# Layer-1 attention output computed transposed, with V stationary in two column halves

## The chip, the cores and the metric

The kernel runs on one core of one Trainium2 chip. The time is that of one execution on the device, in microseconds (us). Lower is better. The kernel before takes 1022.87 us, the median of three runs (1020.79 to 1023.86).

## The reference, cut to what matters

Two transformer layers on x of shape (32, 128, 128): cross-attention and a feed-forward part in each. The change touches the second attention (layer 1) and, at one place, the feed-forward part behind it.

```python
def _L1_xattn_ref(x, context, mask, ...):
    h, d = 16, 64; scale = h ** (-0.5)
    xn = _ln(x, ln1_s, ln1_b); cn = _ln(context, lnc_s, lnc_b)
    q = xn @ Wq; k, v = jnp.split(cn @ Wkv, 2, axis=-1)        # to 16 heads of 64
    k = concatenate(null_kv[0], k); v = concatenate(null_kv[1], v)
    sim = einsum('bhid,bhjd->bhij', q * scale, k); sim = where(mask, sim, -max)
    attn = softmax(sim, axis=-1)
    out = einsum('bhij,bhjd->bhid', attn, v) -> (b, n, 1024)
    return _ln(out @ Wo, lno_s, lno_b)

x = x + _L0_xattn(_layernorm(x), ctx); x = x + _L0_moe_ffn(_layernorm(x))
x = x + _L1_xattn_ref(_layernorm(x), ctx, mask, ...)
x = x + _L1_ffn(_layernorm(x))        # gate, up, down with quantised weights and activations
```

There is one null key and value ahead of the 128 keys of each sequence, so a softmax runs over 129 entries.

## The kernel before

All four parts run on one core, written by hand engine by engine; semaphores tie the engines together. Layer 0 (attention with routing, then the experts) takes the first 400 us or so. The rest is `attention_ffn_block` (from L1080), which this change is in. Its tensors have 128 partitions; one iteration b handles one sequence of 128 rows, and the engines run ahead of each other: iteration b does scores and softmax of sequence b, prepares queries and keys of b + 1, writes out the attention of b - 1, and does the feed-forward part of sequence f = b - 3.

The order of the work on each engine is fixed by the loops at the end of `tensor_part` (PE, L1593), `scalar_part` (ACT, L1708), `vector_part` (DVE, L1914), `pool_part` (POOL, L1333) and `sync_part` (SP's DMA queue, L1228). An engine does its list strictly in turn, so an instruction that waits holds all behind it.

PSUM has eight banks. Two (`maxp`) take the low-precision scores for the row maxima, two (`tp`) the scores proper, two (`op`) the product of the softmax with V, and the last two, `pa` and `pb`, are shared by all that remains: queries, keys, values, transposes, gate, up, down and output. Who may write `pa` or `pb` next is told by waits, such as this one in `queries(b, half)` (L1438), whose second half writes `pb`, which `gate_multiply(b - 4)` reads as its second operand:

```python
            elif b >= 4:
                pe.wait_ge(gt_ready, b - 3)
```

The attention of one sequence goes as follows. `scores` (L1506) leaves keys on partitions and rows of x along the free axis, for 8 heads at a time, in pairs that use the upper and the lower half of the rows of PE's array. `exps` on ACT turns them into `pT`. `weighted` (L1521) multiplies for each head with pT as the stationary operand (128 x 128) and V of this head with a mask column behind it as the moving one (65 columns); the extra column is the sum over keys. `normalise` on DVE (L1784), in three chunks of heads, adds the null entry `pn`, takes the reciprocals of 6, 5 and 5 sums and multiplies. The result `oh` has rows of x on partitions, so `o_transposes` on PE (L1420) turns it by 8 transposes, `o_copy` on ACT (L1671) moves it to `oT`, and `output` (L1471) multiplies by Wo. The weights of the null entry take a transpose (L1415) and a copy (L1652) of their own. `null_scores` (L1463) is the score of the null key, one small matmul into bank `op[0]`.

In the feed-forward part, `gate_part` (L1553) writes `pb`, `gate_tanh` on ACT (L1687) and `gate_multiply` on DVE (L1870) read it; `up_part` writes `pa`, read by `multiply`; then `h_range`, `h_scale` on ACT, `h_round` on DVE (L1893) and `h_transposes` on PE (L1571), `h_copy` and `down`. `quantise_x` (L1853), `out_norm` (L1813), `stats` (L1737) and `norm` (L1750) are small 128 x 128 steps of DVE. `k_copy` (L1759) moves half the keys out of PSUM. Layer 0's product with V (`values`, L365) has 32 columns of V stationary and writes four heads into four quarters of the partitions.

## Time and profile before

| | before |
|---|---|
| median of three runs | 1022.87 us |
| the profiled execution, its own time | 1026.15 us |
| its span | 1024.3 us |
| PE busy | 946.9 us (92%) |
| PE weight loads | 775.3 us (76%) |
| DVE busy | 724.9 us (71%) |
| ACT busy | 464.1 us (45%) |
| POOL busy | 405.9 us (40%) |
| mean granted clock of PE | 0.97 |

The busy time of PE is the union of its matmuls; they are pipelined, so the duration of one record overlaps the next, and what counts is the distance between starts. An f32 matmul leaves two records, a bf16 matmul and an f32 transpose one. Shapes such as 128*64 behind a tile are the part of the array (rows * columns) that holds the weights. "Idle before" with an arrow names what released the engine.

### The profile page before, as it was taken

The page shows a single profiled execution, that of the slowest core. Times are in us where ns is not written, and L with a number is a line of the kernel's source. Part 1 is how long each engine was busy: PE and PEld are TensorE (multiplying, and loading weights), DVE is VectorE, ACT ScalarE, POOL GpSimd, SP SyncE. Part 2 cuts the span into 40 slices and gives each one's busy share as a digit, 9 for nine tenths or more (in the row PEclk, how much of TensorE's full clock was granted, in tenths as well). Part 3 has the DMA queues.
Part 4 walks back from the last instruction along what each step waited for, and adds up shares of the span by engine and source line. Part 5 has one row for each costly group of instructions (what it writes and reads, how often), then busy time and mean ns, then how long its engine had stood idle before and what let it go on. Part 6 is the DMA issues. An engine that isn't in the chain of part 4 may idle for free.

```text
span 1024.3 us, 27291 instructions
## 1 busy us (share of the span) xinstructions
PE 946.9 (92%) x9480; PEld 775.3 (76%) x9510; DVE 724.9 (71%) x2240; ACT 464.1 (45%) x1073; POOL 405.9 (40%) x993
## 2 busy tenths in 40 slices
PE   4999999999689994899999999999999999999973
PEld 2677776777578884788888888888888888888851
DVE  2577777777543553668888788888878878788764
ACT  1355454454325652343545445444454544445432
POOL 3243467655632224242434435343343434434121
PEclk9999999999889997899999999999999999999995
DMA  8555400000355663000000000000000000000000
GB/s 218 179 200 199 171 18 18 12 8 12 98 153 153 165 160 86 12 12 7 9 17 10 17 9 16 11 9 17 10 17 9 10 17 9 17 10 7 4 6 8
DMA packets 47880, 54.23 MB, mean 53 GB/s; under 512 B 6658, under 2 KB 32642, under 8 KB 47746
## 3 DMA queue, kind: packets, MB, share of 16 engines
q1 hardware_dynamic: 33746, 28.43, 10.3%
q10 hardware_dynamic: 11952, 19.86, 5.2%
q0 software_dynamic: 2048, 4.20, 1.4%
q8 instruction: 78, 1.28, 0.5%
q14 instruction: 56, 0.46, 0.2%
HBM read 28.36 MB, written 24.12 MB: 51 GB/s over the span
## 4 chain that ended last, share of the span: by engine, by line
PE 89%; DVE 4%; issue 2%; SPq 2%; DMA 1%; ACT 1%; POOL 1%; DVEq 0%; POOLq 0%; ACTq 0%
PE psum L1548 11%; PE psum L354 7%; PE psum L1512 7%; PE psum L1460 6%; PE psum L1452 6%; PE psum L1493 6%; PE psum L1478 5%; PE psum L872 4%; PE psum L361 4%; PE psum L1517 3%; PE psum L371 3%; PE psum L862 3%; PE psum L1434 3%; PE psum L1502 2%; PE psum L344 2%
## 5 line engine op out<-in xcount | busy, mean ns | idle before, releaser
L1548 PE MATMUL psum<-a_v,a_pT 128*128 128x65 f32 x1024 | 124.1, 274 | 0.1
L1548 PEld LDWEIGHTS psum<-a_v,a_pT 128*128 128x128 f32 x1024 | 119.7, 192 | 1.2
L468 ACT ACTIVATE l_pT<-psum 128x512 f32<-128x512 f32 x128 | 69.7, 595 | 71.7 <-PE psum L361 71.5
L589 DVE TENSOR_REDUCE l_mx<-psum 128x4 bf16<-128x512 f32 x128 | 82.1, 683 | 12.8 <-PE psum L344 12.0
L1317 POOL TENSOR_TENSOR f_hd<-f_hmc,f_wmean 128x1 f32<-128x1 f32 x32 | 6.1, 192 | 197.3 <-DVE f_hr L1891 197.3
L1775 DVE TENSOR_REDUCE a_mxf<-psum 128x4 f32<-128x512 f32 x128 | 81.2, 676 | 0.0
L1460 PEld LDWEIGHTS psum<-a_cTm,a_Wk 128*128 128x128 f32 x512 | 63.4, 195 | 21.7 <-issue 21.7
L1664 ACT ACTIVATE a_pT<-psum 128x512 f32<-128x512 f32 x128 | 69.5, 599 | 20.7 <-PE psum L1517 20.7
L1452 PEld LDWEIGHTS psum<-a_xT,a_Wq 128*128 128x128 f32 x512 | 66.2, 196 | 16.3 <-issue 14.8
L354 PE MATMUL psum<-l_qz,l_kT 32*128 32x256 f32 x512 | 76.2, 417 | 0.0
L1512 PE MATMUL psum<-a_qT,a_kT 64*128 64x128 f32 x1024 | 75.3, 287 | 0.0
L1763 DVE TENSOR_TENSOR a_kT<-psum,a_nkm 128x512 f32<-128x512 f32 x64 | 44.0, 688 | 40.4 <-PE psum L1460 40.4
L1460 PE MATMUL psum<-a_cTm,a_Wk 128*128 128x128 f32 x512 | 72.4, 286 | 0.0
L1452 PE MATMUL psum<-a_xT,a_Wq 128*128 128x128 f32 x512 | 70.8, 283 | 1.1 <-ACT a_cT L1648 1.1
L1674 ACT COPY a_oT<-psum 128x512 f32<-128x512 f32 x64 | 37.4, 585 | 75.6 <-PE psum L1434 75.6
L1512 PEld LDWEIGHTS psum<-a_qT,a_kT 64*128 64x128 f32 x1024 | 62.9, 189 | 10.6 <-issue 10.5
L1493 PE MATMUL psum<-a_Wv,a_cTm 128*128 128x512 f32 x128 | 67.3, 608 | 0.6 <-DVE f_x L1903 0.5
L1478 PE MATMUL psum<-a_Wo,a_oT 128*128 128x128 f32 x512 | 63.2, 277 | 3.4 <-DVE f_h L1880 3.4
L1478 PEld LDWEIGHTS psum<-a_Wo,a_oT 128*128 128x128 f32 x512 | 60.3, 193 | 3.7 <-issue 3.7
L1684 ACT COPY a_v<-psum 128x512 f32<-128x512 f32 x64 | 37.5, 586 | 53.8 <-PE psum L1493 53.8
L354 PEld LDWEIGHTS psum<-l_qz,l_kT 32*128 32x128 f32 x512 | 45.7, 192 | 12.8 <-issue 4.8
L831 POOL COPY e_w2t<-e_w 128x512 f32 x39 | 23.8, 614 | 75.6 <-PE psum L872 75.6
(289 smaller groups left out, 2212.0 us busy)
## 6 DMA issues: line engine op xcount, KB each, us to landing
sorted_x<-r_zeros ACTq DMA_DIRECT2D x12, 1408.0 KB, 5.5
e_w<-in_E_W1b SPq DMA_DIRECT2D x39, 258.0 KB, 2.8
e_xt<-sorted_x SPq DMA_DIRECT2D x39, 64.0 KB, 2.3
sorted_y<-e_yt ACTq DMA_DIRECT2D x39, 64.0 KB, 2.3
a_cin<-in_ctx SPq DMA_DIRECT2D x32, 64.0 KB
out<-f_x SPq DMA_DIRECT2D x32, 64.0 KB, 1.7
x_res<-in_x SPq DMA_DIRECT2D x1, 512.0 KB, 5.8
l_cT<-in_ctxT SPq DMA_DIRECT2D x1, 512.0 KB, 7.0
```

What stands on the lines that cost most here:

```text
L354: nc.tensor.matmul(tp[e][:, 2 * n * S:2 * (n + 1) * S], kT[r, s, :], qz[r, s, 2 * n:2 * n + 2, :].rearrange("p h q -> p (h q)"), start=(n ...
L468: nc.scalar.activation(pT[:, k, :], tp[k % 2], ACT.Exp, scale=SCALE).then_inc(exp_ready, 1)
L589: nc.vector.tensor_reduce(mx[:, s, Q4 * k:Q4 * k + Q4], maxp[k % 2].rearrange("p (h t) -> p h t", h=Q4), AX_X, ALU.max).then_inc(mx_ready, 1)
L1452: last = nc.tensor.matmul(bank[:, i * S:(i + 1) * S], Wq[:, 4 * half + i, :], xT[:, b % 2, :], start=True, stop=True)
L1460: last = nc.tensor.matmul(bank[:, i * S:(i + 1) * S], Wk[:, 4 * half + i, :], cTm[:, b % 2, :], start=True, stop=True)
L1478: nc.tensor.matmul(pa[:, 0:D], oT[:, p, :], Wo[:, p, :], start=(p == 0), stop=False)
L1493: nc.tensor.matmul(bank, cTm[:, b % 2, :], Wv[:, 512 * half:512 * half + 512], start=True, stop=True).then_inc(v_done, 1)
L1512: nc.tensor.matmul(tp[e][:, i * S:(i + 1) * S], kT[r, b % 2, p, :], qT[r, b % 2, p, :], start=(i == 0), stop=False, skip_group_check=True)
L1548: mm = nc.tensor.matmul(op[c][:, k * VW:k * VW + HD + 1], pT[:, hh // 4, (hh % 4) * S:(hh % 4 + 1) * S], v[:, b % 2, hh, :], start=True, s ...
L1664: nc.scalar.activation(pT[:, 2 * half + e, :], tp[e], ACT.Exp, scale=SCALE).then_inc(exp_ready, 1)
L1763: nc.vector.tensor_tensor(kT[:, b % 2, 4 * half:4 * half + 4, :], (pa, pb)[half].rearrange("p (n k) -> p n k", n=4), nkm[:, b % 2, :].unsq ...
L1775: nc.vector.tensor_reduce(mxf[:, hh:hh + 4], maxp[e].rearrange("p (h t) -> p h t", h=Q4), AX_X, ALU.max).then_inc(mxf_ready, 1)
```

## The change

- `weighted`: V of a head (128 x 64) is now stationary and pT (128 columns) moves; the even and the odd group of heads go to the lower and the upper 64 partitions of one bank, so the output comes out transposed. V loses its mask column. `o_transposes`, `o_copy`, the transpose of `wn` and its copy are gone. Wo is loaded with its rows in the order of the new layout.
- `sums`: 16 matmuls with a mask block of 32 columns stationary sum pT over keys into four quarters of the partitions, 4 more transpose the null entries `pn`. Both go to a corner of bank `maxp[0]`.
- `null_copy` on ACT, and `inverse` on DVE (an add and a reciprocal of 128 x 128).
- `spread` on SP: the 16 rows of reciprocals are stored to DRAM and loaded back to all partitions (two DMAs of 256 KB).
- `normalise` on DVE is now two multiplications of 128 x 512, one iteration later, ahead of `gate_multiply`.
- POOL takes over the residual add, the rounding of h and the null weights. `null_scores` moves to another bank and place. On SP's queue, context tiles are loaded and outputs stored behind `spread`.

```diff
@@ tiles
-    v = sb("v", [P, 2, H, HD + 1])
+    v = sb("v", [P, 2, H, HD])
+    mask_sel = sb("mask_sel", [P, 2, Q4, Q4 * G])
-    dn, pn = sb("dn", [P, H]), sb("pn", [P, H])
+    dn, pn = sb("dn", [P, H]), sb("pn", [P, H, G])
+    nullT, denT, rT = sb("nullT", [P, S]), sb("denT", [P, S]), sb("rT", [P, S])
+    r_all = sb("r_all", [P, 2, Q4 * S])
+    denP, nullP = maxp[0][:, 0:S], maxp[0][:, S:2 * S]
+    r_rows = nc.dram_tensor("a_r_rows", (H, S), F32, kind="Internal").ap()
@@ SP
+        def spread(b):
+            sp.wait_ge(inverse_seq, 2 * b + 2)
+            if b >= 1:
+                sp.wait_ge(r_spread, 32 * b)
+            sp.dma_start(r_rows, rT[0:P:G, :]).then_inc(r_stored, 16)
+            sp.wait_ge(r_stored, 16 * (b + 1))
+            if b >= 1:
+                sp.wait_ge(oT_ready, 2 * b)
+            for e in range(2):
+                rows = r_rows.rearrange("(a e i) q -> e a (i q)", a=2, e=2)[e]
+                sp.dma_start(r_all[e * HD:(e + 1) * HD, :, :], rows.partition_broadcast(HD)).then_inc(r_spread, 16)
-        for b in range(2, B):
-            context(b)
-            if b >= 8:
-                store(b - 8)
+        for b in range(B):
+            spread(b)
+            if b + 4 < B:
+                context(b + 4)
+            if b >= 4:
+                store(b - 4)
@@ POOL
+        def residual(b):
+            slot_wait(g, y_in, b)
+            nc.gpsimd.tensor_tensor(x_res[:, b, :], x_res[:, b, :], y[:, b, :], ALU.add).then_inc(x2_ready, 1)
+        def hidden_round(f):
+            g.wait_ge(ht_ready, f + 1)
+            wait(g, htr_done, f)
+            nc.gpsimd.tensor_scalar(hq[:], ht[:], -M, 127.0, ALU.add, ALU.min).then_inc(hq_ready, 1)
+        def null_weights(b):
+            g.wait_ge(inverse_seq, 2 * b + 2)
+            wait(g, out_done, b - 1)
+            nc.gpsimd.tensor_tensor(wT[:, b % 2, :], nullT[:], rT[:], ALU.mult).then_inc(wT_ready, 1)
@@ PE
-        def o_transposes(b, half):
...
         def null_scores(b):
-            nc.tensor.matmul(op[0][:, SN], xT[:, b % 2, :], Wn[:], start=True, stop=True).then_inc(sn_done, 1)
+            pe.wait_ge(xT_ready, b + 1)
+            if b < 5:
+                pe.wait_ge(kT_ready, 2 * max(b, 1))
+            else:
+                pe.wait_ge(hqT_ready, b - 4)
+            nc.tensor.matmul(pb[:, SN], xT[:, b % 2, :], Wn[:], start=True, stop=True).then_inc(sn_done, 1)
         def weighted(b, half):
-            for hh in range(8 * half, 8 * half + 8):
...
-                mm = nc.tensor.matmul(op[c][:, k * VW:k * VW + HD + 1], pT[:, hh // 4, (hh % 4) * S:(hh % 4 + 1) * S], v[:, b % 2, hh, :],
-                                      start=True, stop=True)
+            pe.wait_ge(exp_ready, 4 * b + 2 * half + 2)
+            pe.wait_ge(v_ready, 2 * b + half + 1)
+            wait(pe, oT_ready, 2 * (b - 1) + half + 1)
+            for i in range(Q4):
+                for e in range(2):
+                    last = nc.tensor.matmul(op[half][e * HD:(e + 1) * HD, i * S:(i + 1) * S], v[:, b % 2, 8 * half + 4 * e + i, :],
+                                            pT[:, 2 * half + e, i * S:(i + 1) * S], start=True, stop=True)
+            last.then_inc(pv_done, 1)
+        def sums(b):
+            pe.wait_ge(exp_ready, 4 * b + 4)
...
+            pe.wait_ge(mxf_ready, 4 * b + 5 if b + 1 < B else 4 * b + 3)
+            for i in range(Q4):
+                for j in range(Q4):
+                    nc.tensor.matmul(denP[32 * j:32 * j + 32, :], mask_sel[:, b % 2, i, :], pT[:, j, i * S:(i + 1) * S],
+                                     start=(i == 0), stop=(i == Q4 - 1), skip_group_check=True)
+            for j in range(Q4):
+                last = nc.tensor.matmul(nullP[32 * j:32 * j + 32, :], pn[:, Q4 * j:Q4 * j + Q4, :].rearrange("p h g -> p (h g)"), ident[:],
+                                        start=True, stop=True, skip_group_check=True)
+            last.then_inc(sums_done, 1)
@@ PE, order of one iteration
+            if more:
+                null_scores(b + 1)
-            if prior:
-                o_transposes(b - 1, 0)
             if here:
                 scores(b, 1)
-            if prior:
-                o_transposes(b - 1, 1)
             if f is not None:
                 gate_part(f)
             if more:
                 max_scores(b + 1, 0)
             if here:
-                weighted(b, 0)
                 values(b, 1)
             if more:
                 queries(b + 1, 1)
             if f is not None:
                 up_part(f)
             if here:
+                weighted(b, 0)
+                sums(b)
                 weighted(b, 1)
@@ ACT
-        def o_copy(b, half):
...
+        def null_copy(b):
+            act.wait_ge(sums_done, b + 1)
+            wait(act, wT_ready, b)
+            nc.scalar.copy(nullT[:], nullP).then_inc(nullT_ready, 1)
@@ DVE
+        def inverse(b):
+            dve.wait_ge(sums_done, b + 1)
+            dve.wait_ge(nullT_ready, b + 1)
+            nc.vector.tensor_tensor(denT[:], denP, nullT[:], ALU.add).then_inc(inverse_seq, 1)
...
+            nc.vector.reciprocal(rT[:], denT[:]).then_inc(inverse_seq, 1)
+        def normalise(b, half):
+            dve.wait_ge(pv_done, 2 * b + half + 1)
+            dve.wait_ge(r_spread, 32 * (b + 1))
+            wait(dve, out_done, b)
+            nc.vector.tensor_tensor(oT[:, 4 * half:4 * half + 4, :].rearrange("p n q -> p (n q)"), op[half], r_all[:, half, :],
+                                    ALU.mult).then_inc(oT_ready, 1)
@@ DVE, order of one iteration
+            if more:
+                sn_copy(b + 1)
             if 2 <= b < B + 2:
                 out_norm(b - 2)
...
             if 2 <= b < B + 2:
                 quantise_x(b - 2)
+            if 1 <= b <= B:
+                normalise(b - 1, 0)
+                normalise(b - 1, 1)
             if f is not None:
                 gate_multiply(f)
-            if here:
-                normalise(b, 0)
-            if more:
-                sn_copy(b + 1)
...
             if here:
-                normalise(b, 1)
-            if f is not None:
-                h_round(f)
+                inverse(b)
             if more:
                 k_copy(b + 1, 1)
-            if here:
-                normalise(b, 2)
-                null_weights(b)
```

On PE, from the gate matmul to the down transposes of one iteration, before (L1434 is o_transposes, L1561 the gate, L1464 null_scores, L1548 weighted, L1493 values, L1452 queries, L1569 up):

```order
L1434 MATMUL psum<-ident,a_oh 128x128 [waits a_kT_ready]
L1434 MATMUL psum<-ident,a_oh 128x128 x3
L1561 MATMUL psum<-f_wq,f_xqT 128x512 [waits a_oT_ready,f_xqT_ready]
L1502 MATMUL psum<-a_kT,a_qT 128x128 [waits a_mxf_ready,a_kT_ready,a_qT_ready]
L1502 MATMUL psum<-a_kT,a_qT 128x128 x7
L1464 MATMUL psum<-a_Wn,a_xT 128x16 [waits a_oh_ready,a_vm_ready,a_sn_ready,a_v_ready,a_exp_ready]
L1548 MATMUL psum<-a_v,a_pT 128x65 x4
L1548 MATMUL psum<-a_v,a_pT 128x65 [waits a_exp_ready]
L1548 MATMUL psum<-a_v,a_pT 128x65
L1548 MATMUL psum<-a_v,a_pT 128x65 [waits a_oh_ready]
L1548 MATMUL psum<-a_v,a_pT 128x65
L1493 MATMUL psum<-a_Wv,a_cTm 128x512 [waits a_oT_ready,a_cTm_ready]
L1452 MATMUL psum<-a_xT,a_Wq 128x128 [waits f_gt_ready]
L1452 MATMUL psum<-a_xT,a_Wq 128x128 x3
L1569 MATMUL psum<-f_wq,f_xqT 128x512 [waits a_v_ready,f_xqT_ready]
L1548 MATMUL psum<-a_v,a_pT 128x65 [waits a_v_ready,a_exp_ready]
L1548 MATMUL psum<-a_v,a_pT 128x65 x2
```

In the changed kernel (L1588 is the gate, L1533 max_scores, L1522 values, L1473 queries, L1594 up, L1562 weighted, L1573 and L1576 the sums):

```order
L1588 MATMUL psum<-f_wq,f_xqT 128x512 [waits a_v_ready,f_xqT_ready]
L1533 MATMUL psum<-a_kT,a_qT 128x128 [waits a_mxf_ready,a_kT_ready,a_qT_ready]
L1533 MATMUL psum<-a_kT,a_qT 128x128 x7
L1522 MATMUL psum<-a_Wv,a_cTm 128x512 [waits a_kT_ready,a_cTm_ready]
L1473 MATMUL psum<-a_xT,a_Wq 128x128 [waits f_gt_ready]
L1473 MATMUL psum<-a_xT,a_Wq 128x128 x3
L1594 MATMUL psum<-f_wq,f_xqT 128x512 [waits a_v_ready,f_xqT_ready]
L1562 MATMUL psum<-a_pT,a_v 64x128 [waits a_oT_ready,a_v_ready,a_exp_ready]
L1562 MATMUL psum<-a_pT,a_v 64x128 x7
L1573 MATMUL psum<-a_pT,a_mask_sel 32x128 [waits a_pn_ready,a_mxf_ready,a_sel_ready,a_exp_ready]
L1573 MATMUL psum<-a_pT,a_mask_sel 32x128 x15
L1576 MATMUL psum<-ident,a_pn 32x128 x4
```

The transposes, null_scores and the first half of weighted no longer stand between scores and queries; the wait of queries for gt_ready has stayed.

On DVE, from the second half of quantise_x to the maxima, before (L1865 and L1868 are its last two steps, L1873 is gate_multiply, L1792 to L1796 normalise):

```order
L1865 TENSOR_SCALAR f_xt<-f_xn,f_rc 128x128 [waits f_x_seq]
L1868 TENSOR_SCALAR f_xq<-f_xt 128x128 [waits f_xqT_ready,f_x_seq]
L1873 SCALAR_TENSOR_TENSOR f_gt<-f_th,psum 128x512 [waits f_h_ready,f_th_ready]
L1792 TENSOR_TENSOR a_den<-psum,a_pn 128x6 [waits a_ot_done,a_pn_ready,a_pv_done]
L1794 RECIPROCAL a_rd<-a_den 128x6 [waits a_rd_done]
L1796 TENSOR_TENSOR a_oh<-psum,a_rd 128x384 [waits a_rd_done]
L1769 COPY a_sn<-psum 128x16 [waits a_dn_ready,a_sn_done]
L1775 TENSOR_REDUCE a_mxf<-psum 128x4 [waits a_max_done]
```

In the changed kernel (L1880 and L1883 are the last steps of quantise_x, L1816 is normalise, L1888 gate_multiply):

```order
L1880 TENSOR_SCALAR f_xt<-f_xn,f_rc 128x128 [waits f_x_seq]
L1883 TENSOR_SCALAR f_xq<-f_xt 128x128 [waits f_xqT_ready,f_x_seq]
L1816 TENSOR_TENSOR a_oT<-psum,a_r_all 128x512 [waits a_out_done,a_r_spread,a_pv_done] x2
L1888 SCALAR_TENSOR_TENSOR f_gt<-f_th,psum 128x512 [waits f_h_ready,f_th_ready]
L1793 TENSOR_REDUCE a_mxf<-psum 128x4 [waits a_max_done]
```

The two multiplications of normalise, of the iteration before, now stand ahead of gate_multiply, with a wait for the DMA.

## Rows read from the trace of the kernel before

**Rows 1.** Windows: us; busy of PE, PEld, DVE, ACT, POOL; granted clock; DMA share; GB/s
```profile
700.00:800.00 100.00, 99.26 (x961) 84.79 (x965) 81.97 (x264) 48.58 (x100) 41.46 (x116) 1.00 0.04 12
```

**Rows 2.** Timeline of PE, one iteration: start us, us, engine, line, op, tiles, records
```profile
703.57 0.40 PE L1502 MATMUL psum<-a_kT,a_qT 64*128 64x128 bf16 x8
...
704.17 0.27 PE L1415 MATMUL psum<-ident,a_wn 128*16 128x128 f32 x1
704.28 0.22 PE L1417 MATMUL psum<-identb,f_xq 128*128 128x128 bf16 x1
...
708.09 1.13 PE L1460 MATMUL psum<-a_cTm,a_Wk 128*128 128x128 f32 x8
709.05 0.60 PE L1434 MATMUL psum<-ident,a_oh 128*128 128x128 f32 x4
709.58 1.16 PE L1512 MATMUL psum<-a_qT,a_kT 64*128 64x128 f32 x16
710.67 0.62 PE L1517 MATMUL psum<-negI,a_mx 128*128 128x128 bf16 x8
...
711.89 0.40 PE L1502 MATMUL psum<-a_kT,a_qT 64*128 64x128 bf16 x8
712.22 0.40 PE L1464 MATMUL psum<-a_Wn,a_xT 128*128 128x16 f32 x2
712.47 1.98 PE L1548 MATMUL psum<-a_v,a_pT 128*128 128x65 f32 x16
714.28 1.08 PE L1493 MATMUL psum<-a_Wv,a_cTm 128*128 128x512 f32 x2
715.20 1.05 PE L1452 MATMUL psum<-a_xT,a_Wq 128*128 128x128 f32 x8
...
716.34 1.93 PE L1548 MATMUL psum<-a_v,a_pT 128*128 128x65 f32 x16
718.10 1.11 PE L1460 MATMUL psum<-a_cTm,a_Wk 128*128 128x128 f32 x8
719.05 1.95 PE L1478 MATMUL psum<-a_Wo,a_oT 128*128 128x128 f32 x16
...
721.67 0.40 PE L1502 MATMUL psum<-a_kT,a_qT 64*128 64x128 bf16 x8
```

**Rows 3.** Timeline of DVE in the same iteration
```profile
709.25 0.69 DVE L1763 TENSOR_TENSOR a_kT<-psum,a_nkm 128x512 f32<-128x512 f32 x1 [0.89 <-PE psum L1460]
709.86 0.34 DVE L1755 TENSOR_SCALAR a_xn<-x_res,a_mv,a_rs 128x128 f32<-128x128 f32 x1
...
711.83 0.26 DVE L1868 TENSOR_SCALAR f_xq<-f_xt 128x128 bf16<-128x128 f32 x1
713.12 0.69 DVE L1873 SCALAR_TENSOR_TENSOR f_gt<-f_th,psum 128x512 f32<-128x512 f32 x1 [1.04 <-ACT f_th L1691]
```

**Rows 4.** Timeline of PE in layer 0, one pair of products with V
```profile
201.59 0.65 PE L371 MATMUL psum<-l_pT,l_v 128*32 128x128 f32 x16
202.17 0.39 PE L316 MATMUL psum<-r_waffT,r_xnT 128*128 128x8 f32 x2
```

**Rows 5.** Groups of DVE instructions to 450 us: count, busy us, mean ns
```profile
L595 DVE RECIPROCAL l_rden<-psum 128x16 f32<-128x16 f32 x32 | 8.2, 256 | 23.4 <-PE psum L381 23.4
...
L549 DVE RECIPROCAL r_tmp<-r_den 128x32 f32<-128x32 f32 x8 | 2.6, 324 | 0.8 <-POOL r_den L240 0.8
```

**Rows 6.** Timelines of PE and of DVE at the end of the run
```profile
998.31 2.65 PE L1478 MATMUL psum<-a_Wo,a_oT 128*128 128x128 f32 x16 [3.43 <-DVE f_h L1880]
...
1011.41 0.43 DVE L1896 TENSOR_SCALAR f_hq<-f_ht 128x512 bf16<-128x512 f32 x1 [0.88 <-ACT f_ht L1698]
```

**Rows 7.** One group of POOL instructions in the whole run
```profile
L1269 POOL TENSOR_SCALAR a_nkm<-a_mask_row,a_nk_neg,a_nk_col 128x128 f32<-128x128 bf16 x32 | 15.3, 479 | 0.1
```

**Rows 8.** The page's DMA issues: count, KB each, us to landing
```profile
out<-f_x SPq DMA_DIRECT2D x32, 64.0 KB, 1.7
...
l_cT<-in_ctxT SPq DMA_DIRECT2D x1, 512.0 KB, 7.0
```

More of the change, by code:

```diff
@@ L1326, in pool_part @@
         null_keys(0)
+        g.wait_ge(f_set, 2)
         mask_columns(0)
@@ L1348, in pool_part @@
                 gather(b + 4)
+            if b + 3 < B:
+                residual(b + 3)
             if 2 <= b < B + 2:
@@ L1352, in pool_part @@
                 out_scale(b - 3)
+                hidden_round(b - 3)
+            if b < B:
+                null_weights(b)
     class Setup:
@@ L1360, in prepare @@
                 rows = slice(j * HD, (j + 1) * HD)
-                nc.vector.tensor_copy(nv_blocks[rows, j::H + 2], nv_col[rows, :].broadcast_to([HD, NP])).then_inc(nv_set, 1)
+                for a in range(2):
+                    first = a * (Q4 * P + NP * G) + j * Q4 * G
+                    nc.vector.tensor_copy(nv_blocks[rows, first:first + 3 * (P + G) + 1:P + G],
+                                          nv_col[rows, :].broadcast_to([HD, Q4])).then_inc(nv_set, 1)
         def tensor(self, pe, bank_free):
@@ L1413, in transposes @@
                 last = nc.tensor.transpose(pa[:, S:2 * S], cn[:, b % 2, :], ident[:])
-            if bw is not None:
-                last = nc.tensor.transpose(pa[0:H, 2 * S:3 * S], wn[:], ident[:])
             if f is not None:
@@ L1418, in transposes @@
             last.then_inc(tr_done, 1)
-        def o_transposes(b, half):
-            bank = (pb, pa)[half]
-            if half == 0:
-                pe.wait_ge(oh_ready, 3 * b + 3)
-                if b + 1 < B:
-                    pe.wait_ge(v_ready, 2 * (b + 1) + 1)
-                else:
-                    pe.wait_ge(x4_ready, B - 3)
-            elif b + 2 < B:
-                pe.wait_ge(kT_ready, 2 * (b + 2) + 1)
-            else:
-                pe.wait_ge(tr_free, b + 1)
-                pe.wait_ge(xqT_ready, b - 1)
-            for i in range(4):
-                last = nc.tensor.transpose(bank[:, i * S:(i + 1) * S],
-                                           oh[:, 8 * half + 2 * i:8 * half + 2 * i + 2, :].rearrange("p h d -> p (h d)"), ident[:])
-            last.then_inc(ot_done, 1)
         def queries(b, half):
@@ L1498, in max_scores @@
             wait(pe, mxf_ready, 2 * (2 * b + half))
+            if half == 1:
+                wait(pe, inverse_seq, 2 * b - 1)
             for i in range(4):
@@ L1649, in xc_copy @@
                 last.then_inc(cT_ready, 1)
-            if bw is not None:
-                wait(act, out_done, bw)
-                nc.scalar.copy(wT[:], pa[0:H, 2 * S:3 * S]).then_inc(tr_free, 1)
             if f is not None:
@@ L1708, in scalar_part @@
         for b in range(B + 3):
-            more, here, prior = b + 1 < B, b < B, 1 <= b <= B
+            more, here = b + 1 < B, b < B
             f = b - 3 if b >= 3 else None
-            if more or prior or f is not None:
-                xc_copy(b, b + 1 if more else None, b - 1 if prior else None, f)
+            if more or f is not None:
+                xc_copy(b, b + 1 if more else None, f)
             if here:
@@ L1731, in scalar_part @@
                 q_copy(b + 1, 1)
+            if here:
+                null_copy(b)
             if f is not None:
```

189 lines of the change are left out of this document (71 added, 118 removed).

## The prediction

> **What bounds the kernel now.** I read the busy time of each engine over one stretch of 100 us first. In the layer-1 steady state TensorE (PE) is busy for 99.26 of 100 us at full granted clock, 2.4 GHz, VectorE (DVE) for 82 and ScalarE (ACT) for 49 [rows 1]. Then I read the timeline of PE over one iteration [rows 2]: every group of matmuls starts when the one before has been issued, and from one max_scores(b, 1) to the next it is 721.67 - 703.57 = 18.10 us. I take "pitch" as start of a group to start of the next, since the durations overlap. So 31 such iterations are PE's own work, and a change counts by what it takes from or adds to that row of pitches, and by any wait that it opens in it. Third, the timeline of DVE [rows 3] for the step that PE may come to wait for.
>
> **What PE loses.** The o_transposes: the first four have a pitch of 709.58 - 709.05 = 0.53; the second four the same, so 1.06. The transpose of wn: 704.28 - 704.17 = 0.11. The 16 weighted matmuls with 65 moving columns: 714.28 - 712.47 = 1.81 and 718.10 - 716.34 = 1.76. Together 4.74 us an iteration [rows 2]. null_scores (0.25, from 712.22 to 712.47) is only moved, to a place ahead of down.
>
> **What PE gains.** 16 weighted matmuls of 128x64 weights with 128 moving columns, in pairs that fill the two column halves. No row of this kernel has two column halves. Nearest is scores, which runs pairs in two row halves, f32 with 128 moving columns: 8 matmuls in 710.67 - 709.58 = 1.09 us [rows 2]. Above lies the full-width matmul of keys, 4 in 709.05 - 708.09 = 0.96, so 1.92 for 8, if halves don't overlap; below lies layer 0's product with V in four column quarters, 8 in 202.17 - 201.59 = 0.58 [rows 4]. I take 1.09 for each half, 2.18 for both. The sums over keys are 16 + 4 matmuls in exactly that form of quarters: 20 x 0.58 / 8 = 1.45 (the upper end, without overlap, is 20 x 0.24 = 4.8; the rows of layer 0 exclude it as likely). PE's own work becomes 18.10 - 4.74 + 2.18 + 1.45 = 16.99 us, 1.11 less.
>
> The Trainium skill (TensorEngine Tiling (Array Packing), Performance Considerations) recommends this very step: where the streamed operand has at most 64 columns, swap it with the stationary one and use column halves, up to twice as fast. Half of the full-width matmul would be 0.96 in place of 1.09 for each half; by that estimate the sum below would be 1036 and not 1044. The row halves of this kernel stay 0.13 above that limit, so I go by them.
>
> **The wait that opens.** queries(b+1, 1) writes bank pb, and for b+1 >= 4 waits for gt_ready: gate_multiply(f) must have read pb. Before, PE issued the end of keys(b+1, 0) at 709.05 and came to queries(b+1, 1) at 715.20, 6.15 us later; DVE had started gate_multiply at 713.12 for 0.69, so it was done at 713.81, 1.4 us early [rows 2, 3]. The change shortens one side and lengthens the other. On PE, both o_transposes (1.06), weighted(b, 0) (1.81) and null_scores (0.25) no longer stand between: 6.15 - 3.12 = 3.03 us. On DVE, k_copy(b+1, 0) starts at 709.25 once PE has done the keys (DVE had sat idle 0.89 us for it, so nothing that gets lighter earlier on DVE helps); from there to the start of the last step of quantise_x it is 711.83 - 709.25 = 2.58, that step 0.26 with its pitch about 0.25. Then come the two new normalise, 128x512 from PSUM with an SBUF operand, the same form as k_copy, whose pitch is 709.86 - 709.25 = 0.61: 1.22 in all. Only then gate_multiply, 0.69. From the issue end of the keys: 0.20 + 2.58 + 0.25 + 1.22 + 0.69 = 4.94 us. Before, gate_multiply sat 1.04 us for ACT's tanh [rows 3]; that cover goes, as the gate matmul comes some 1.1 us earlier and DVE arrives 1.22 later. So PE stands 4.94 - 3.03 = 1.91 us before queries(b+1, 1), in each of 28 iterations (queries of 4 to 31). The wait isn't absorbed elsewhere: keys(b+2, 0) follow it on PE with no slack, and they release the next k_copy. The period is a cycle: 16.99 + 1.91 = 18.90 us, 0.80 more than 18.10.
>
> **What else moves, and why it costs nothing.** After sums(b): a copy of nullT on ACT (a 128x128 block from PSUM, estimated under 0.69, the time of DVE's 128x512), an add (about 0.3), and a reciprocal of 128x128 on DVE. Reciprocals of 16 and 32 elements took 256 and 324 ns [rows 5], 4.25 ns an element more, so about 0.73 for 128; at most four times 324 = 1.3. That ends some 1.8 us after the sums. k_copy(b+1, 1) is queued behind it, and its keys are issued 1.09 + 0.95 = 2.04 after the sums; PE asks for it at h_transposes, after another 2.3 of output. DVE also loses the three divisions, the residual add and the rounding, so it is no bound. The rounding of h goes to GpSimd (POOL): DVE took 0.43 [rows 6], the nearest POOL row has 479 ns for 128x128 [rows 7], four times that is 1.9; I take 1.2. It follows h_scale (DVE waited 0.88 us for it there), which itself follows the copy of nullT: 0.5 + 0.9 + 1.2 = 2.6 after the sums, at worst 3.3, and h_transposes come at 4.3. POOL's residual add (0.48 by the same row) and null_weights lie in its idle time, 59 of 100 us [rows 1]. The reciprocals' way by DMA: from there to normalise(b, 0) in the next iteration there are 1.09 + 3.57 (keys to max_scores [rows 2]) + 5.62 (max_scores to the end of keys, with null_scores in and wn out) + 3.03 = 13.3 less 1.8, or 11.5 us. A store takes 1.7 to land and 512 KB took 7.0 [rows 8]; the broadcast is 2 x 256 KB, so 8.7, on SP's queue ahead of context(b+4) and store(b-4), whose users come an iteration later.
>
> **Ends.** Iterations 0 to 2 have no gt wait: 3 x -1.11 = -3.3. POOL's residual add and fills stand ahead of the first rsqrt: +0.5, an estimate by its 0.48 for 128x128. At the end PE is no bound: iteration 31 is 1.1 shorter, the two normalise (1.2) come onto the chain of iteration 32, and two roundings on POOL (2 x 0.8) onto the last two: +1.7. Sum: 28 x 0.80 - 3.3 + 0.5 + 1.7 = +21.3 us. Against the profiled execution, 1026.15, that is 1047.5; against the median of 1022.87, which is 3.3 below it, **1044 us**.
>
> **Rivals.** (A) *The gate wait does not bind, the kernel is faster.* It decides at one point: whether gate_multiply ends less than 3.03 us after the keys are issued. Then the time is 31 x -1.11 + 2.2 = -32, **991**. For it: PE is the bound at 99% and loses 4.74 for 3.63. Against it: the steps ahead of the two normalise alone take 0.20 + 2.58 + 0.25, which is all of the 3.03 [rows 3]. Chance 0.10; a tie (a wait near 1.1, within 0.3%, which is about what a measurement of this kernel can tell from no change) 0.03. (B) *The column halves do not overlap*: 2 x (1.92 - 1.09) = 1.66 x 31 = 51 more, **1095**; against it, quarters do overlap. 0.07. (C) *The spread reciprocals land late*, as a new bound in place of the gate: 2 us past the 11.5 would give 30 x 2, **1104**. Small broadcast pieces have no row here; against it are 2.8 us of slack. 0.06. (D) *The clock falls after each wait.* After 3.43 us of idle the 16 records of output took 2.65 against 1.95 [rows 2, 6]. If each wait costs about 3 us at 1.2 GHz, 1.1 x 28 = 31 more, **1075**; against it, 1.9 us is well short of 3.43. 0.05. (That the change does not do what it says is case B.)
>
> **How the numbers follow.** The forecast has 0.69. Its own bounds come mostly from the weighted matmuls (0.58 to 1.92 a half, -32 to +51 over the run); taking the half of that nearest to the row of scores, it runs from about 1022 up to 1070. The range reaches to D and into the lower part of B and C, and leaves A out: 1022 to 1085, with 2 in 10 outside. Faster 0.10, same 0.03, slower 0.87.
>
> **What would show it.** PE waits before queries(b+1, 1), released by DVE's gate_multiply, about 1.9 us each, 28 times; period 18.9; PE busy near 90% at full clock; weighted 1.1 for 8, sums about 1.45; DVE's k_copy to gate_multiply without a gap; normalise released by its own queue and not by DMA. It would be wrong if PE stayed at 99% (A, or B if the period is over 19.5), if normalise waited for DMA (C), or if granted clock fell below 1.00 (D).

## The result, and the profile after

| | before | after |
|---|---|---|
| median (runs beside each other) | 1023.37 us (1020.79 to 1025.29, 4 runs) | 1037.16 us (1031.46 to 1039.97, 4 runs) |
| profiled execution, its span | 1026.15, 1024.3 us | 1034.68, 1033.0 us |
| PE busy | 946.9 us | 909.1 us |

The ratio is 1.0129, 95% interval 1.0075 to 1.0184: slower by 13.8 us. Forecast were +21 (1044), a range of 1022 to 1085 and 0.87 for slower. The side and the mechanism hold; most sizes came out smaller, and one at the end larger. The two profiled executions differ by 8.7 us of span, and 12 further runs of the changed kernel, below, give a ratio of 1.008, so 13.8 is the upper part of what the change costs.

The page's first part after the change:

```profile
PE 909.1 (88%) x10472; PEld 716.0 (69%) x10502; DVE 704.4 (68%) x1986; ACT 428.6 (41%) x1009; POOL 499.3 (48%) x1091
```

PE has 38 us less to do, and the kernel takes longer: that time, and more, is now waiting. PE's longest waits after the change (waited for: us in total, times, longest):

```profile
PE psum L1473 <- DVE f_gt L1888: 41.8, 28, 1.7
PE psum L1601 <- POOL f_hq L1338: 14.9, 2, 9.0
...
PE psum L1504 <- DVE f_h L1895: 6.3, 1, 6.3
```

L1473 is `queries`, L1888 `gate_multiply`: the predicted wait, in the predicted 28 iterations. The other two lie at the end of the run. The window of [rows 1], after the change (same columns):

```profile
700.00:800.00 100.00, 91.72 (x1116) 74.26 (x1118) 76.47 (x212) 41.67 (x89) 56.67 (x126) 1.00 0.18 45
```

PE was busy for 99.26 us here and is for 91.72, in this stretch without any loss of clock. One iteration of PE, which answers to [rows 2]:

```profile
704.11 0.40 PE L1533 MATMUL psum<-a_kT,a_qT 64*128 64x128 bf16 x8
...
708.72 1.13 PE L1481 MATMUL psum<-a_cTm,a_Wk 128*128 128x128 f32 x8
709.77 1.16 PE L1543 MATMUL psum<-a_qT,a_kT 64*128 64x128 f32 x16
...
711.97 1.12 PE L1522 MATMUL psum<-a_Wv,a_cTm 128*128 128x512 f32 x2
714.61 1.16 PE L1473 MATMUL psum<-a_xT,a_Wq 128*128 128x128 f32 x8 [1.51 <-DVE f_gt L1888]
715.60 0.38 PE L1594 MATMUL psum<-f_wq,f_xqT 128*128 128x512 bf16 x1
715.91 1.09 PE L1562 MATMUL psum<-a_pT,a_v 128*64 128x128 f32 x16
716.94 1.08 PE L1573 MATMUL psum<-a_pT,a_mask_sel 128*32 128x128 f32 x32
717.83 0.40 PE L1576 MATMUL psum<-ident,a_pn 128*32 128x128 f32 x8
718.16 1.09 PE L1562 MATMUL psum<-a_pT,a_v 128*64 128x128 f32 x16
719.19 1.16 PE L1481 MATMUL psum<-a_cTm,a_Wk 128*128 128x128 f32 x8
720.18 1.95 PE L1504 MATMUL psum<-a_Wo,a_oT 128*128 128x128 f32 x16
721.97 0.39 PE L1506 MATMUL psum<-a_NO,a_wT 128*128 128x128 f32 x2
...
722.51 0.40 PE L1533 MATMUL psum<-a_kT,a_qT 64*128 64x128 bf16 x8
```

The period is 722.51 - 704.11 = 18.40 us. `values(b, 1)` (711.97) has a pitch of 2.64 where the same two matmuls otherwise have 0.94 (707.78 to 708.72), so the wait costs 1.70 us of the period; the row's "1.51 idle" is less by the overlap of records. PE's own work is 18.40 - 1.70 = 16.70. What the wait is for, on DVE, which answers to [rows 3]:

```profile
709.88 0.69 DVE L1781 TENSOR_TENSOR a_kT<-psum,a_nkm 128x512 f32<-128x512 f32 x1 [0.96 <-PE psum L1481]
...
712.40 0.36 DVE L1883 TENSOR_SCALAR f_xq<-f_xt 128x128 bf16<-128x128 f32 x1
712.68 1.27 DVE L1816 TENSOR_TENSOR a_oT<-psum,a_r_all 128x512 f32<-128x512 f32 x2
713.88 0.67 DVE L1888 SCALAR_TENSOR_TENSOR f_gt<-f_th,psum 128x512 f32<-128x512 f32 x1
...
718.99 0.95 DVE L1810 RECIPROCAL a_rT<-a_denT 128x128 f32<-128x128 f32 x1
```

From `k_copy` to the end of `gate_multiply` DVE has no gap. `normalise` is released by nothing but DVE's own queue.

**Where the 8.7 us of span come from.** The starts of the 32 `output` groups (L1478 before, L1504 after) date every iteration. Before, output(0) starts at 447.75 and output(31) at 998.31; after, at 444.99 and 1002.44. So the beginning is 2.8 us shorter, the 31 iterations take 557.45 in place of 550.56 (+6.9), and from output(31) to the end it is 30.6 in place of 26.0 (+4.6). Among the 31 distances, the first has no wait in it (16.11 against 17.94), the second, which has the first wait, took 19.86 against 18.36, most of the others 18.40 against 18.07. Summed up, against before: first distance -1.8, second +1.5, the 25 after it +8.0, the last four -0.8, together +6.9. The beginning should not be read as the change's work: over the executions profiled here, of all kernels, output(0) starts anywhere from 438 to 459 us, as layer 0 ends earlier or later. It is probably much of the scatter between runs, which is not shown, since most kernels have one profiled execution only; it is the reason why the experiments are read by output(0) to output(31) beside the medians.

The second iteration is longer by the clock. PE waited 1.60 us at 473.78, and then the same groups took up to 1.7 times as long (start, us, group):

```profile
468.85 1.16 PE L1543 MATMUL psum<-a_qT,a_kT 64*128 64x128 f32 x16
...
473.78 1.77 PE L1473 MATMUL psum<-a_xT,a_Wq 128*128 128x128 f32 x8 [1.60 <-DVE f_gt L1888]
475.90 1.88 PE L1562 MATMUL psum<-a_pT,a_v 128*64 128x128 f32 x16
478.94 1.09 PE L1562 MATMUL psum<-a_pT,a_v 128*64 128x128 f32 x16
```

Windows of that stretch (busy time of PE, PEld, DVE, ACT, POOL; granted clock):

```profile
470.00:475.00 5.00, 3.25 (x27) 2.20 (x27) 4.79 (x13) 2.14 (x4) 2.10 (x5) 0.91 0.05 13
475.00:480.00 5.00, 5.00 (x77) 3.77 (x76) 2.39 (x7) 1.51 (x3) 0.19 (x1) 0.74 0.02 3
```

The windows before and after these two have 1.00. A mean of 0.74 is a mixture: about half of that window at 1.2 GHz, the rest at 2.4. The kernel below with the residual add moved kept its clock there and took 18.14, with a wait shorter by 0.11; so the fall cost 19.86 - 18.14 - 0.11 = 1.6 us.

The end of the run, PE and POOL, which answers to [rows 6] and [rows 7]:

```profile
1002.44 3.75 PE L1504 MATMUL psum<-a_Wo,a_oT 128*128 128x128 f32 x16 [6.30 <-DVE f_h L1895]
...
1018.12 0.61 PE L1601 MATMUL psum<-identb,f_hq 128*128 128x128 bf16 x4 [9.02 <-POOL f_hq L1338]
...
1027.45 0.61 PE L1601 MATMUL psum<-identb,f_hq 128*128 128x128 bf16 x4 [5.89 <-POOL f_hq L1338]
```
```profile
1016.12 1.95 POOL L1338 TENSOR_SCALAR f_hq<-f_ht 128x512 bf16<-128x512 f32 x1 [0.66 <-ACT f_ht L1720]
```

Here nothing covers POOL: 1.95 - 0.43 = 1.5 us more in each of the last two roundings, 3.0 together. The kernel below with the rounding on DVE confirms it: from output(31) to the last four transposes of h it takes 21.91 us, where the changed kernel takes 25.01 and the kernel before 21.36. output(31) comes after 6.30 us without work, in place of 3.43, and takes 3.75 in place of 2.65 at a lower clock (granted 0.67 in 1000 to 1010); about half of that is made up by the small groups behind it, and 0.5 is left, since the kernel with the rounding on DVE has the same 3.75. Up to those transposes that is 3.7 of the 4.6. The other 0.9 lies behind the last DVE instruction, in the store of the last output, and stays open.

### The profile page after: what moved, and what is told of

The parts are those of the page before. It is cut to its first block and busy times, and to the rows that moved or that the text cites. A ratio compares the mean times of both kernels' runs of the same rounds, so it can differ in the third digit from the quotient of the medians.

```text
span 1033.0 us, 29281 instructions
## 1 busy us (share of the span) xinstructions
PE 909.1 (88%) x10472; PEld 716.0 (69%) x10502; DVE 704.4 (68%) x1986; ACT 428.6 (41%) x1009; POOL 499.3 (48%) x1091
## 3 DMA queue, kind: packets, MB, share of 16 engines
q10 hardware_dynamic: 11952, 19.86, 5.2%
## 5 line engine op out<-in xcount | busy, mean ns | idle before, releaser
L1473 PE MATMUL psum<-a_xT,a_Wq 128*128 128x128 f32 x512 | 75.3, 293 | 42.9 <-DVE f_gt L1888 41.8
L1473 PEld LDWEIGHTS psum<-a_xT,a_Wq 128*128 128x128 f32 x512 | 65.2, 199 | 67.9 <-DVE f_gt L1888 65.0
L1338 POOL TENSOR_SCALAR f_hq<-f_ht 128x512 bf16<-128x512 f32 x32 | 62.3, 1946 | 37.8 <-ACT f_ht L1720 37.8
L1562 PE MATMUL psum<-a_pT,a_v 128*64 128x128 f32 x1024 | 70.8, 281 | 0.0
L1504 PE MATMUL psum<-a_Wo,a_oT 128*128 128x128 f32 x512 | 64.3, 280 | 6.3 <-DVE f_h L1895 6.3
L1522 PE MATMUL psum<-a_Wv,a_cTm 128*128 128x512 f32 x128 | 68.8, 620 | 0.6 <-DVE f_x L1913 0.5
L1562 PEld LDWEIGHTS psum<-a_pT,a_v 128*64 128x64 f32 x1024 | 55.4, 138 | 16.0 <-issue 15.8
L1504 PEld LDWEIGHTS psum<-a_Wo,a_oT 128*128 128x128 f32 x512 | 61.4, 196 | 6.9 <-issue 6.9
L1702 ACT COPY a_qT<-psum 128x512 f32<-128x512 f32 x64 | 37.4, 585 | 67.1 <-PE psum L1473 66.8
L1725 ACT COPY f_hqT<-psum 128x512 bf16<-128x512 bf16 x32 | 18.7, 585 | 104.1 <-PE psum L1601 104.1
```

What stands on the lines that cost most here:

```text
L1338: nc.gpsimd.tensor_scalar(hq[:], ht[:], -M, 127.0, ALU.add, ALU.min).then_inc(hq_ready, 1)
L1473: last = nc.tensor.matmul(bank[:, i * S:(i + 1) * S], Wq[:, 4 * half + i, :], xT[:, b % 2, :], start=True, stop=True)
L1504: nc.tensor.matmul(pa[:, 0:D], oT[:, p, :], Wo[:, p, :], start=(p == 0), stop=False)
L1522: nc.tensor.matmul(bank, cTm[:, b % 2, :], Wv[:, 512 * half:512 * half + 512], start=True, stop=True).then_inc(v_done, 1)
L1562: last = nc.tensor.matmul(op[half][e * HD:(e + 1) * HD, i * S:(i + 1) * S], v[:, b % 2, 8 * half + 4 * e + i, :], pT[:, 2 * half + e, i * ...
```

## The experiments

All are edits of the changed kernel unless another base is named. The ratio is to the kernel before, run beside each (medians 1022.69 to 1024.62). Period is the usual distance of two `output` groups; "31 iterations" is output(0) to output(31) of the profiled execution; the wait is that of `queries` for `gate_multiply` in the list of waits.

| kernel | median us | ratio to before [95%] | period | 31 iterations | wait, us in total |
|---|---|---|---|---|---|
| before | 1023.37 | | 18.07 | 550.6 | none |
| after | 1037.16 | 1.0129 [1.0075, 1.0184] | 18.40 | 557.4 | 41.8 |
| after, once more | 1033.57 | 1.008 [1.0049, 1.0112] | 18.41 | 559.5 | 42.2 |
| gate first | 1001.25 | 0.9765 [0.9713, 0.9816] | 17.21 | 522.7 | 8.7 |
| extra DVE work | 1090.5 | 1.064 [1.0599, 1.068] | 20.48 | 613.0 | 58.8 |
| no spread | 1037.24 | 1.0115 [1.0063, 1.0166] | 18.40 | 557.3 | 41.7 |
| rounding on DVE | 1050.03 | 1.0263 [1.0235, 1.0291] | 18.58 | 574.3 | 45.9 |
| both orders | 987.61 | 0.9654 [0.963, 0.9678] | 16.91 | 514.5 | none |
| halves apart | 1028.41 | 1.007 [1.0043, 1.0098] | 18.18 | 551.7 | 8.7 |
| 16 null rows | 1012.0 | 0.9875 [0.9847, 0.9904] | 17.51 | 531.9 | 9.0 |
| extra work, gate first | 1016.92 | 0.9972 [0.9936, 1.0009] | 17.82 | 542.4 | 25.2 |
| residual add later | 1023.52 | 1.0015 [0.9994, 1.0036] | 18.28 | 552.5 | 38.6 |
| before, extra DVE work | 1023.73 | 1.0015 [0.9977, 1.0053] | 18.07 | 551.5 | none |

The theory: the period is PE's own work, smaller than before, plus a wait for `gate_multiply`, opened because the change takes work off PE between the keys and `queries(b+1, 1)` and puts the two `normalise` ahead of `gate_multiply`. Rivals: the wait belongs to the DMA of the reciprocals; the column halves do not overlap; DVE's longer path would cost the time whatever PE does.

**The changed kernel once more.**

> The changed kernel once more, unchanged, to see how far its time and its clock scatter. Theory (PE waits for gate_multiply in each of 28 iterations): median within 1031 to 1040, iterations of 18.40 us, 1.5 us of waiting before queries(b+1, 1) each time. Rival (the clock falls after some of the waits, and that makes part of the loss): iterations above 18.4 with a granted clock under 1.00 in them, more of them where the run is longer.

With 12 runs the ratio is 1.008, so together with the first comparison the change costs 8 to 14 us. In this execution two iterations took 19.93 and 20.20, in place of one, each after a wait in which the clock fell.

**Gate first.**

```diff
+            if f is not None:
+                gate_multiply(f)
             if 1 <= b <= B:
                 normalise(b - 1, 0)
                 normalise(b - 1, 1)
-            if f is not None:
-                gate_multiply(f)
```

> gate_multiply(f) ahead of the two normalise on DVE, nothing else moved. Theory: the two multiplications (1.20 us) leave the path from keys to queries, the wait falls from 1.5 to about 0.3 and the iteration from 18.40 to 17.2; 28 x 1.2 = 34 us less, about 1003, faster than both kernels. Rival 1 (the order on DVE does not matter, PE's own work is the bound): 18.4 stays, 1037. Rival 2 (the wait moves on: weighted(b, 0) then waits for normalise, or the sums for the maxima): a gain under 15 us.

PE and DVE of this kernel:

```profile
714.77 1.12 PE L1522 MATMUL psum<-a_Wv,a_cTm 128*128 128x512 f32 x2
716.22 1.16 PE L1473 MATMUL psum<-a_xT,a_Wq 128*128 128x128 f32 x8 [0.33 <-DVE f_gt L1888]
```
```profile
715.21 0.36 DVE L1883 TENSOR_SCALAR f_xq<-f_xt 128x128 bf16<-128x128 f32 x1
715.49 0.68 DVE L1888 SCALAR_TENSOR_TENSOR f_gt<-f_th,psum 128x512 f32<-128x512 f32 x1
716.09 1.28 DVE L1816 TENSOR_TENSOR a_oT<-psum,a_r_all 128x512 f32<-128x512 f32 x2
```

No work is removed, two steps change places, and the wait's share of the period goes from 1.70 to 0.51 (1.45 - 0.94): 1.19, the two `normalise` (1.20). The period follows, 18.40 to 17.21, and the kernel is 32 us faster than the changed kernel run again and 22 to 23 faster than before. That settles what the change lost by: the same swap of operands in another order is a gain.

**Extra DVE work**, one unused multiplication of 128x512 between `normalise` and `gate_multiply`:

```diff
                 normalise(b - 1, 1)
+            if 1 <= b <= B:
+                nc.vector.tensor_tensor(spare[:], r_all[:, 0, :], r_all[:, 1, :], ALU.mult)
             if f is not None:
```

> One more DVE multiplication of 128x512 in SBUF, whose result nobody uses, between normalise and gate_multiply. Theory: its whole pitch of about 0.6 us comes onto the iteration, 19.0, and 28 x 0.6 = 17 us onto the time, about 1054; the wait of PE grows from 1.5 to 2.1. Rival (PE's own work is the bound, DVE has 24% idle time): nothing, 1037.

The period rose by 2.07, not by the 0.6 of the instruction, and the time by 57 us in place of the 17 expected. PE at the first wait, and after one in the middle:

```profile
472.07 1.16 PE L1474 MATMUL psum<-a_xT,a_Wq 128*128 128x128 f32 x8 [2.27 <-DVE f_gt L1889]
...
716.88 2.07 PE L1474 MATMUL psum<-a_xT,a_Wq 128*128 128x128 f32 x8 [2.13 <-DVE f_gt L1889]
...
719.31 1.43 PE L1563 MATMUL psum<-a_pT,a_v 128*64 128x128 f32 x16
721.90 1.09 PE L1563 MATMUL psum<-a_pT,a_v 128*64 128x128 f32 x16
```

`queries` takes 2.07 in place of 1.16, the first `weighted` 1.43 in place of 1.09; the granted clock is 0.91 to 0.93 in every window of 20 us from 480 to 1020. So 26 of the 28 iterations with the wait lose 0.6 to the instruction and about 1.5 to the clock. The two others keep their clock: the last, after a wait of 1.47, and the first, after the longest wait of all (2.27); it took 18.93, and the granted clock in 470 to 490 is 1.00. The prediction's rival D is a real mechanism, with this much more to wait for, but the length of the wait alone does not decide it.

**No spread.** The DMAs of the reciprocals are left out, `normalise` multiplies by a tile of constants, and the output is no softmax:

```diff
         for b in range(B):
-            spread(b)
```

> The reciprocals are not stored and spread by DMA; normalise multiplies by a constant tile filled once, so the output is not the softmax's. Theory (the DMA lies beside other work): iterations stay at 18.4, the time within 3 us of the changed kernel. Rival (the spread is late, or its 512 KB per iteration slow DVE or PE by contention for SBUF): a shorter iteration, a gain over 10 us.

557.3 against 557.4 us, wait 41.7 against 41.8, median 1037.24 against 1037.16: DRAM and back costs nothing. This rules out rival C.

**Rounding on DVE.** `hidden_round` leaves POOL and becomes `h_round` on DVE, ahead of `k_copy(b+1, 1)`, as before the change.

```diff
             if here:
                 inverse(b)
+            if f is not None:
+                h_round(f)
             if more:
                 k_copy(b + 1, 1)
```

> The rounding of h back from POOL to DVE (ahead of k_copy(b+1, 1)), all else as changed. Theory (it costs only at the end of the run, where no other sequence hides it): iterations stay at 18.40, the end gets some 3 us shorter, since two roundings there take 0.43 and not 1.95. Rival (POOL's 1.95 us hold back the next iteration's POOL work and so the steady state): iterations under 18.3, more than 8 us.

The end did get shorter, 26.4 us from output(31) in place of 30.6. For the iterations the expectation was wrong, and so for the whole in sign: 14.8 us more over the 31 iterations than the changed kernel run again. DVE and POOL ahead of the wait:

```profile
703.43 0.57 DVE L1879 TENSOR_SCALAR f_xt<-f_xn,f_rc 128x128 f32<-128x128 f32 x1
703.44 0.47 POOL L1268 TENSOR_TENSOR x_res<-x_res,xy 128x128 f32<-128x128 f32 x1
...
706.13 1.16 PE L1472 MATMUL psum<-a_xT,a_Wq 128*128 128x128 f32 x8 [1.69 <-DVE f_gt L1887]
```

Without the rounding POOL gets to its residual add earlier, and that now runs beside a step of `quantise_x` on DVE, which takes 0.57 in place of 0.29. (In the changed kernel the add, at 712.20 to 712.67 of its trace, ran beside the step after that one, at 712.40, which took 0.36 there and 0.25 here; that takes back 0.10.) The wait grows from 1.51 to 1.69, the period to 18.58, and nine iterations, with waits of 1.60 to 1.69, are longer still (19.87 to 20.19): the clock falls after the wait, in place of once or twice.

**Residual add later**, on the last kernel, to try just that:

```diff
-            if b + 3 < B:
-                residual(b + 3)
             if 2 <= b < B + 2:
                 hidden_scales(b - 2)
             if b >= 3:
                 out_scale(b - 3)
+            if b + 3 < B:
+                residual(b + 3)
```

> The rounding on DVE as in e4, and POOL's residual add put behind its two small scale steps, so that it no longer runs beside DVE's second step of quantise_x. Theory (in e4 that step took 0.57 instead of 0.29 because POOL's add ran beside it; the wait grew by this much, from 1.5 to 1.69, and at 1.69 the clock falls in every third iteration): the step takes 0.29 again, iterations of 18.40, one or two clock falls, about 1030, 20 us less than e4. Rival (the rounding on DVE is itself what costs the 17 us of e4): 1050 stays.

DVE, POOL and PE:

```profile
703.88 0.29 DVE L1879 TENSOR_SCALAR f_xt<-f_xn,f_rc 128x128 f32<-128x128 f32 x1
...
706.28 1.16 PE L1472 MATMUL psum<-a_xT,a_Wq 128*128 128x128 f32 x8 [1.38 <-DVE f_gt L1887]
```
```profile
709.78 0.46 POOL L1268 TENSOR_TENSOR x_res<-x_res,xy 128x128 f32<-128x128 f32 x1
```

The add stands elsewhere, the DVE step is back at 0.29, the wait is 1.38, the period 18.28, and no iteration is over 18.38. The 31 iterations are 21.8 us shorter than in the kernel above: the 9 that kept their clock this time are 1.7 to 1.9 shorter each (some 17 us), the others 0.30 (some 5). The two profiled executions differ by 30.0 us: these 21.8 and 8.1 at the start (440.0 against 448.1); the medians differ by 26.5. So an add of 0.47 us on an engine that is idle for more than half the time moves the kernel by 2%, through DVE's step, the wait and the clock. It also cost the changed kernel something: there the period is 18.40 and the wait 1.51, 0.12 and 0.13 more than here, and the step beside the add takes 0.36 in place of 0.23.

**Both orders.** DVE takes `normalise`, then `gate_multiply`, both ahead of `quantise_x`; PE does `weighted(b, 0)` ahead of `queries(b+1, 1)`; the rounding is on DVE behind `k_copy(b+1, 1)`.

```diff
             if here:
                 values(b, 1)
+                weighted(b, 0)
             if more:
                 queries(b + 1, 1)
             if f is not None:
                 up_part(f)
             if here:
-                weighted(b, 0)
                 sums(b)
```

> On DVE normalise and gate_multiply both ahead of quantise_x, on PE weighted(b, 0) ahead of queries(b+1, 1), the rounding on DVE. Theory (once nothing makes PE wait, its own work of 16.9 us is the iteration): 28 x 1.5 = 42 us less and 3 us at the end, about 990. Rival (another step of DVE, made late by the new order, holds PE: k_copy(b+1, 1) or the maxima ahead of the sums): iterations of 17.2 or more, 1000 or above.

The same part of DVE's row:

```profile
706.33 1.28 DVE L1815 TENSOR_TENSOR a_oT<-psum,a_r_all 128x512 f32<-128x512 f32 x2
707.79 0.69 DVE L1887 SCALAR_TENSOR_TENSOR f_gt<-f_th,psum 128x512 f32<-128x512 f32 x1 [0.18 <-ACT f_th L1712]
```

`gate_multiply` is done at 708.48, `queries` comes at 709.39, DVE waits a little for the tanh again, as in [rows 3]. 987.61 us is 35 less than before and the best of all. Without a wait the period is PE's own work in this order, 16.91 and not 16.70: `values(b, 1)`, now ahead of `weighted`, has a pitch of 1.06 in place of 0.94, and `up_part`, now ahead of the sums, 0.40 in place of 0.31. What each of the changes of order gives by itself was not tried.

**Extra work, gate first**: an unused multiplication of 128x512 ahead of `gate_multiply`, in the kernel with the gate first.

> The unused DVE multiplication of 128x512 once more ahead of gate_multiply, but on top of gate_multiply first, where PE waits only 0.33 us. Theory (e2 cost 57 us because its longer wait also made the clock fall in each iteration; without that the multiplication costs its own 0.6 us): the wait grows to 0.9, the iteration to 17.8, 28 x 0.6 = 17 us, about 1018, granted clock 1.00 throughout. Rival (the multiplication itself costs more than its duration, by traffic in SBUF or by another wait): 2 us an iteration as in e2, about 1055.

The period grows by 0.61 (17.21 to 17.82), the wait is 0.92, and the granted clock stays at 1.00 in every window of 20 us from 420 to 960. A multiplication of the same size (its operands are another tile) that cost 2.07 an iteration on top of a wait of 1.51 costs its own pitch on top of one of 0.33. So the other 1.5 of the first trial are the clock's.

**Before, extra DVE work**: the kernel before, with two unused multiplications of 128x512 ahead of `gate_multiply`.

> The kernel before with two unused 128x512 multiplications on DVE ahead of gate_multiply, some 1.2 to 1.4 us in all, the same place and the same load as the two normalise of the change, and nothing else changed. Theory (the swap opens the wait because it takes PE's work out of the stretch between keys and queries(b+1, 1), not because DVE got more work): gate_multiply was done 1.4 us before PE asked, and it also waited 1.04 us for tanh, which hides most of the additions; so the period stays at 18.1 to 18.2, with no wait over 0.1 before queries, and the time within 0.5% of before. Rival (DVE's longer path costs the time by itself): waits of about 1 us before queries, period 18.9 to 19.3, time 1045 to 1060.

```profile
710.74 0.68 DVE L1939 TENSOR_TENSOR a_spare<-a_spare 128x512 f32<-128x512 f32 x1
711.34 0.68 DVE L1940 TENSOR_TENSOR a_spare<-a_spare 128x512 f32<-128x512 f32 x1
711.94 0.68 DVE L1876 SCALAR_TENSOR_TENSOR f_gt<-f_th,psum 128x512 f32<-128x512 f32 x1
```

DVE got the load of the two `normalise` in their place, and the period stays at 18.07: the wait for the tanh went, PE came to `queries` at 713.93, 1.3 us after. The longer path on DVE is harmless by itself; it needs PE's shorter one beside it.

**Halves apart**, on the kernel with the gate first: four heads of the lower half, then four of the upper, in place of by turns.

```diff
-            for i in range(Q4):
-                for e in range(2):
+            for e in range(2):
+                for i in range(Q4):
```

> On top of gate_multiply first: the eight matmuls of weighted are issued four for the lower column half and then four for the upper, not in turn. Theory (two halves overlap only when neighbours in the order go to different halves): 8 take about 1.9 and not 1.03, 2 x 0.87 x 31 = 54 us more than gate_multiply first, about 1055. Rival (64-column matmuls are quick by themselves, whatever their order): 1.03 and no difference, 1001.

```profile
708.75 1.58 PE L1562 MATMUL psum<-a_pT,a_v 128*64 128x128 f32 x16
710.26 1.08 PE L1573 MATMUL psum<-a_pT,a_mask_sel 128*32 128x128 f32 x32
```

710.26 - 708.75 = 1.51 for 8 matmuls, against 1.03 by turns and 1.92 for 8 of full width by [rows 2]. By turns the halves do overlap; apart they still lie below the full-width price, which the expectation did not have. The period grew by 0.97, 2 x 0.48.

**16 null rows**, on the kernel with the gate first: the last matmul of `output` contracts over 16 partitions of wT and NO instead of 128, which leaves out most of the null entries' part.

> On top of gate_multiply first: the last matmul of output reads only 16 of the 128 partitions of wT and NO, so most null weights are left out of the output. Theory (the changed kernel's output got 0.20 us shorter, 0.22 against 0.42, since this matmul no longer uses 16 rows of the array beside 128 before it): the pitch goes back to 0.42, 0.2 x 31 = 6 us more than gate_multiply first. Rival (the 0.20 come from what follows it): no difference.

```profile
704.62 0.48 PE L1506 MATMUL psum<-a_NO,a_wT 16*128 16x128 f32 x2
705.04 0.40 PE L1601 MATMUL psum<-identb,f_hq 128*128 128x128 bf16 x4
```

This matmul has a pitch of 705.04 - 704.62 = 0.42 with 16 rows of the array and 722.19 - 721.97 = 0.22 with 128, and the 8 ahead of it 1.88 against 1.79: 0.29 in all, by which the period differs (17.51 against 17.21). I had expected 0.20; the 0.09 on the group ahead was new.

## Why the prediction was right, point by point

**PE loses.** The `weighted` part, the transpose of wn and the moved `null_scores` stand. For the `o_transposes` 1.06 was taken; 0.53 + 0.45 = 0.98 went, since the second pitch also held a matmul of the gate (0.31) whose record is missing in [rows 2].

**PE gains.** `weighted` measured 1.03 for 8 (716.94 - 715.91), forecast 1.09; the sums 0.89 + 0.33 = 1.22, forecast 1.45. By the factor of 2 that the Trainium skill (TensorEngine Tiling (Array Packing), Performance Considerations) gives for column halves, an estimate is 0.96, half of the full width. The trace's 1.03 stays 0.07 above it, about midway to the row halves that I went by. Not foreseen: `output` became 2.01 from 2.30, since the null weights now fill 128 rows of the array (shown by the run with 16), and four groups cost more: keys(b+1, 0) 1.05 from 0.96, `up_part` 0.31 from 0.21, the second keys 0.99 from 0.95, `queries` 0.99 from 0.93. The first three now have a group in halves of the array beside them, where before it was one on the whole array; `queries` has not. That the change between whole array and halves is the cause was not tried by itself. Own work is 16.70, forecast 16.99, so PE gained 1.4 us an iteration.

**The wait.** From the start of the keys to the start of `queries`, DVE's path was forecast as 0.96 + 4.94 = 5.90 and measured 714.61 - 708.72 = 5.89. PE's was forecast as 0.96 + 3.03 = 3.99 and measured as 711.97 + 0.94 - 708.72 = 4.19, 0.09 of the difference by the keys' 1.05 and 0.08 by the `o_transposes`. So the wait is 1.70, forecast 1.91. Both errors, 0.29 and 0.21, have the same sign: the period is 18.40 in place of 18.90. From keys to `queries` DVE sets the time, so only what PE does from `queries` on to the next keys counts: 18.40 - 5.89 = 12.51 us, forecast 18.90 - 5.90 = 13.00, and this is where the 0.5 went. This is the term of the sum that was mis-sized: 28 x 0.80 = 22 us were forecast, and the period came out 0.33 over before, which gives 8 us over the 25 distances that have it whole. A difference of 0.80 between 18.90 and 18.10 could not bear an error of 0.5.

**Sizes too small.** The reciprocal of 128x128 took 0.95, forecast 0.73; the rounding on POOL 1.95, forecast 1.2 with an upper end of 1.9, which was exceeded. Neither shows in the steady state. At the end the rounding does: +4.6 in place of +1.7, the sum's term "two roundings on POOL (2 x 0.8)" being 3.0, while the lower clock after the longer idle stretch (0.5) and the 0.9 behind the last DVE instruction had no term.

**The rest.** Where no wait stands yet, from output(0) to output(1), PE gained more than the 1.11 forecast (16.11 against 17.94). The spread cost nothing in the steady state, as forecast. POOL's residual add, said to lie in its idle time, cost 0.12 us an iteration by the run with the add moved, since it ran beside a DVE step on the way to `gate_multiply`. The start cannot be told from the scatter of layer 0.

**Luck.** The wait, its place and its number were forecast for the right reason. That the total lies as near as it does is partly luck: the steady state gave 8 us of 22, while a fall of the clock (+1.5), the larger end and the scatter of the first comparison (13.8, where the profiled executions say 8.7) made up for some of it.

**The rivals.** A fell: `gate_multiply` was 1.7 us late in every iteration. B and C were excluded by a run each. D has a part: one or two iterations of the changed kernel lose 1.5 to 1.8 us to the clock. The argument against it, that 1.9 us was well short of the 3.43 in [rows 6], does not hold: with 0.6 us more to wait the clock fell in 26 of 28 iterations. With the 1.91 forecast, D deserved more than 0.05. Its price was too low as well: 3 us at half the clock do the work of 1.5, so they lose 1.5 and not 1.1, and 1.5 to 1.8 is what a fall cost.
